# Attention's DVE and ACT order changed, its first batch normalised in halves, some of the final weighing moved to DVE, one batch's statistics moved

## What is computed

```python
x = x + 0.5 * ffn(layernorm(x))
x = x + attention(layernorm(x))
x = x + 0.5 * ffn(layernorm(x))          # the same weights as the first

def ffn(x):                               # 16 experts, top 2 of the 2 best of 4 groups, inner width 128
    s = softmax(x @ gate_w.T); pick 2 of s + gate_b in the two best groups; weights = s of the picked
    return sum over the 2 of weight * ((silu(x @ We1 + be1) * (x @ We3 + be3)) @ We2 + be2) \
         + (silu(x @ ws1 + bs1) * (x @ ws3 + bs3)) @ ws2 + bs2

def attention(x):                         # 16 heads of 16, linear attention
    q, k, v = relu(x @ Wq), relu(x @ Wk), x @ Wv
    z = 1 / (sum_n(k) . q + eps)
    return ((v^T k) q * z) @ w_proj.T + b_proj
```

## Time and profile before

| | |
|---|---|
| median of 3 runs | 1249.27 us (1247.13 to 1252.63) |
| the profiled execution | 1243.24 us, its span 1241.5 us |
| PE busy (matmul) | 1148.4 us, 93% |
| DVE busy | 852.7 us, 69% |
| ACT busy | 759.6 us, 61% |
| POOL busy | 698.1 us, 56% |
| DMA, mean | 146 GB/s; about 400 GB/s in the final stage |
| granted TensorE clock, mean | 0.982 of full |

### The profile page before, as it was taken

One profiled execution on the slowest core, in us unless ns is written; L12 is line 12 of the kernel. 1 busy time (PEld: TensorE's weight loads), 2 busy tenths in 40 slices (PEclk: granted clock), 3 DMA queues, 4 the chain that ended last, 5 costly groups with the idle time before them and its releaser, 6 DMA issues.

```text
span 1241.5 us, 26349 instructions
## 1 busy us (share of the span) xinstructions
PE 1148.4 (93%) x6696; PEld 904.6 (73%) x6696; DVE 852.7 (69%) x2774; ACT 759.6 (61%) x1698; POOL 698.1 (56%) x850
## 2 busy tenths in 40 slices
PE   7988999999999967899998999889998999999995
PEld 5555555899999946777887878545557999999653
DVE  6788784566666655768878786677844666666488
ACT  4454441688888845675655653544415888888398
POOL 3577776488888854000411503356763888887810
PEclk9999999999999998999999999899999999999997
DMA  9922227556555523012320400114585555555398
GB/s 360 309 91 95 98 104 201 172 172 174 171 172 156 164 104 105 32 38 68 112 72 24 133 22 35 35 69 141 171 210 180 173 170 174 173 157 162 119 400 333
DMA packets 94215, 181.53 MB, mean 146 GB/s; under 512 B 17624, under 2 KB 60400, under 8 KB 92022
## 3 DMA queue, kind: packets, MB, share of 16 engines
q1 hardware_dynamic: 66630, 110.44, 29.2%
q0 software_dynamic: 26016, 67.55, 15.3%
q10 hardware_dynamic: 1424, 1.86, 0.5%
HBM read 97.63 MB, written 86.08 MB: 148 GB/s over the span
## 4 chain that ended last, share of the span: by engine, by line
PE 58%; DVE 17%; ACT 11%; issue 5%; POOL 5%; DMA 3%; SPq 1%; DVEq 0%; ACTq 0%; POOLq 0%
PE bank L700 20%; PE bank L710 10%; PE bank L559 7%; PE bank L691 5%; POOL expert_rows L1683 4%; PE bank L575 4%; PE bank L806 3%; ACT rows L1021 3%; ACT w L1021 3%; DVE stat L1161 2%; PE bank L756 2%; PE bank L732 2%; ACT xn L1039 1%; PE bank L521 1%; ACT rows L898 1%
## 5 line engine op out<-in xcount | busy, mean ns | idle before, releaser
L700 PE MATMUL bank<-rows,att 128*128 128x128 f32 x2288 | 303.2, 276 | 0.3 <-ACT att L1010 0.3
L700 PEld LDWEIGHTS bank<-rows,att 128*128 128x128 f32 x2288 | 279.2, 192 | 0.8 <-ACT att L1010 0.6
L1683 POOL DMA_INDIRECT expert_rows<-rows,slots x160 | 155.4, 971 | 80.0 <-issue 57.3
L1010 ACT COPY att<-w 128x512 f32 x286 | 177.0, 619 | 10.2 <-issue 4.2
L1740 POOL DMA_INDIRECT routed_rows<-silu,rdest x160 | 158.3, 989 | 35.0 <-issue 24.6
L1458 DVE SCALAR_TENSOR_TENSOR rows<-bank,tile_b,att 128x128 f32<-128x128 f32 x286 | 100.1, 350 | 112.9 <-ACT att L1015 102.0
L710 PE MATMUL bank<-w,rows 128*128 x572 | 171.5, 382 | 4.3 <-DVE rows L1458 4.2
L1740 POOL DMA_INDIRECT routed_rows<-rows,rdest x126 | 124.7, 990 | 68.4 <-DVE rdest L1441 40.7
L1009 ACT COPY rows<-bank 128x256 f32<-128x256 f32 x286 | 106.6, 373 | 89.1 <-PE bank L691 86.9
L575 PE MATMUL bank<-ws,be 128*128 128x256 f32 x512 | 124.0, 388 | 8.6 <-DVE be L1364 8.6
L925 ACT ACTIVATE silu<-bank,bs 128x512 f32<-128x512 f32 x64 | 43.9, 686 | 127.6 <-PE bank L559 117.5
(11 more groups left out here) (212 smaller groups left out, 2156.9 us busy)
## 6 DMA issues: line engine op xcount, KB each, us to landing
rows<-expert_rows SPq DMA_DIRECT2D x286, 129.5 KB
rows<-routed_rows SPq DMA_DIRECT2D x32, 512.0 KB, 4.2
w<-routed_rows SPq DMA_DIRECT2D x10, 1024.0 KB, 10.9
out<-xres SPq DMA_DIRECT2D x16, 512.0 KB, 9.3
xres<-in_x SPq DMA_DIRECT2D x7, 1024.0 KB, 9.5
rows<-routed_rows SPq DMA_DIRECT2D x6, 1024.0 KB, 7.7
expert_rows<-pad SPq DMA_DIRECT2D x47, 129.5 KB, 14.0
w<-in_w SPq DMA_DIRECT2D x1, 4096.0 KB, 24.4
```

What stands on the lines that cost most here:

```text
L700: last = nc.tensor.matmul(rh_ps[t % RB][:, n * P:(n + 1) * P], m.rw13[:, t % RB, c * C + n * INTER:c * C + (n + 1) * INTER], m.rT[:, t % R ...
L1010: nc.scalar.copy(m.rw13[:, a % RB, :].rearrange("p (c n) -> p c n", c=KC), w13[:, :, bass.ds(expert_at(i + 2), C)]).then_inc(s.rw13_copied, 1)
L1683: nc.gpsimd.indirect_dma_start(out=d.xg, out_offset=bass.IndirectOffsetOnAxis(ap=m.slots[:, slots_of(r), k, i:i + 1], axis=0), in_=m.xs[bu ...
```

## The change

- In the attention periods 0 to 6, DVE no longer takes the statistics of the last pair of tiles ahead of the second half of the key sum, but behind it, with the aggregation.
- ACT's last two normalising instructions of a batch (`following(range(6, 8))`) stand behind the second copy of transposed queries, where they stood ahead of the mixer's copy.
- In the first batch the statistics, `rstd`, negated mean, normalising and transposes are done for tiles 0 to 3 first, and for tiles 4 to 7 later: ACT's second half stands behind its second relu, PE's behind the second Gram step. The four weighings of batch 1 stand behind ACT's relus 3 to 6, where they stood behind 0, 2, 4 and 6.
- In period 7, `route_stats(13)` stands behind `route_stats(11)`, ahead of `sum_keys(7, 0)`, with a semaphore of its own; it leaves the period's end.
- In final pieces 3, 7, 11 and 15, DVE weighs and adds the first of the two routed rows in one instruction for each tile (`scalar_tensor_tensor`), and ACT weighs only the second.

```diff
--- before.py
+++ after.py
@@ -291,6 +291,10 @@
 NEXT = BATCHES + EARLY
 
 
+def weighed_by_dve(n):
+    return 1 if n % 4 == 3 else 0
+
+
 def early_in(b, step):
 
     e, late = divmod(b - 1 - step, 2)
@@ -828,8 +834,8 @@
 
             pe.wait_ge(s.att_weights_in, 16 * len(att_loads))
             pe.wait_ge(s.bias_placed, 16)
-            for n in range(4):
-                a_transpose(0, n)
+            a_transpose(0, 0)
+            a_transpose(0, 1)
             keys(0, 0)
             keys(0, 1)
             for b in range(BATCHES):
@@ -843,6 +849,9 @@
                 keys(b, 2)
                 for i in range(NT):
                     gram(b, i)
+                    if b == 0 and i == 1:
+                        a_transpose(0, 2)
+                        a_transpose(0, 3)
                     if i + 3 < NT:
                         keys(b, i + 3)
                     if i == 5:
@@ -1015,8 +1024,8 @@
                         nc.scalar.activation(m.rsilu[:, t % RB, :], rh_ps[t % RB][:, 0:P], ACT.Silu,
                                              bias=m.tile_b13[:, 0, i:i + 1]).then_inc(s.rsilu_ready, 1)
 
-            def weigh(b, tiles, y):
-                for k in range(2):
+            def weigh(b, tiles, y, choices=range(2)):
+                for k in choices:
                     for j, i in enumerate(tiles):
                         last = nc.scalar.activation(y[:, k, j * C:(j + 1) * C], y[:, k, j * C:(j + 1) * C], ACT.Copy,
                                                     scale=m.weights[:, b, k, i:i + 1])
@@ -1030,10 +1039,14 @@
             def weigh_final(n):
                 b, h = divmod(n, PIECES)
                 act.wait_ge(s.f_loaded[n % FSLOTS], 16 * (n // FSLOTS + 1))
-                weigh(b, range(h * NT // PIECES, (h + 1) * NT // PIECES), m.yf[n % FSLOTS]).then_inc(s.f_weighted, 1)
+                weigh(b, range(h * NT // PIECES, (h + 1) * NT // PIECES), m.yf[n % FSLOTS],
+                      range(weighed_by_dve(n), 2)).then_inc(s.f_weighted, 1)
 
             def a_normalise(b, tiles):
-                act.wait_ge(s.a_nmr_ready, b + 1)
+                if b == 0 and tiles[0] < PAIRS:
+                    act.wait_ge(s.a_first_nmr, 1)
+                else:
+                    act.wait_ge(s.a_nmr_ready, b + 1)
                 wait(act, s.g_ready, b)
                 for i in tiles:
                     last = nc.scalar.activation(m.xn[:, i, :], m.xres[:, b, i, :], ACT.Identity,
@@ -1090,9 +1103,9 @@
 
             for h in range(PAIRS):
                 weigh_routed(0, h)
-            a_normalise(0, range(NT))
-            for n in range(4):
-                a_copy_xT(0, n)
+            a_normalise(0, range(0, PAIRS))
+            a_copy_xT(0, 0)
+            a_copy_xT(0, 1)
             for b in range(BATCHES):
                 more = b + 1 < BATCHES
                 fresh, ranked = early_in(b, 0), early_in(b, 1)
@@ -1103,7 +1116,15 @@
 
                 for i in range(NT):
                     relu_k(b, i)
-                    if more and i % 2 == 0:
+                    if b == 0:
+                        if i == 1:
+                            a_normalise(0, range(PAIRS, NT))
+                        if i == 3:
+                            a_copy_xT(0, 2)
+                            a_copy_xT(0, 3)
+                        if 3 <= i < 7:
+                            weigh_routed(1, i - 3)
+                    elif more and i % 2 == 0:
                         weigh_routed(b + 1, i // 2)
                     if fresh is not None and 3 <= i < 7:
                         normalise(fresh, range(2 * i - 6, 2 * i - 4))
@@ -1124,11 +1145,12 @@
                 relu_q(b, 2)
                 following(range(4, 6))
                 relu_q(b, 3)
-                following(range(6, 8))
                 act.wait_ge(s.mixer_ready, b + 1)
                 nc.scalar.copy(m.m_sb.rearrange("p c n -> p (c n)"), g_ps[:]).then_inc(s.mixer_copied, 1)
                 for p in range(PAIRS):
                     copy_qT(b, p)
+                    if p == 1:
+                        following(range(6, 8))
                     if more:
                         a_copy_xT(b + 1, p)
                     else:
@@ -1471,7 +1493,7 @@
                             dve.wait_ge(s.rows_out[last_user % SLOTS], 16 * (last_user // SLOTS) + 16)
                         TT(m.ry[(i - 2) % RYSLOTS], ry_ps[y % RB][:, 0:C], m.be2[:, bass.ds(e, C)], ALU.add).then_inc(s.ry_scaled, 1)
 
-            def combine(b, h):
+            def combine(b, h, measure=True):
                 n = PAIRS * b + h
                 y = m.ylq[:, n % YSLOTS]
                 dve.wait_ge(s.bias_added, BIASED.index(b) + 1)
@@ -1479,7 +1501,11 @@
                 dve.wait_ge(s.weighted, n + 1)
                 ch.then(TT(x, x, y[:, 0, :], ALU.add))
                 TT(x, x, y[:, 1, :], ALU.add).then_inc(s.combined, 1)
-                dve.wait_ge(s.combined, n + 1)
+                if measure:
+                    measure_sums(b, h)
+
+            def measure_sums(b, h):
+                dve.wait_ge(s.combined, PAIRS * b + h + 1)
                 stats(b, range(2 * h, 2 * h + 2))
 
             def a_negate_mean(b):
@@ -1574,10 +1600,14 @@
             for n in HELD[0]:
                 shared(0, n, iter(()), 0)
 
-            for h in range(PAIRS):
+            for h in range(PAIRS // 2):
                 combine(0, h)
-            aggregate(s.a_stats_ready)
-            a_negate_mean(0)
+            half_aggregate(0, s.a_first_stats)
+            combine(0, 2)
+            half_negate_mean(0, s.a_first_rstd, s.a_first_nmr)
+            combine(0, 3)
+            half_aggregate(1, s.a_stats_ready)
+            half_negate_mean(1, s.a_rstd_ready, s.a_nmr_ready)
             def steps(work, count):
                 for _ in range(count):
                     next(work, None)
@@ -1597,7 +1627,9 @@
                         steps(work, 1)
                     combine(b + 1, 1)
                 else:
-                    route_stats(BATCHES + EARLY)
+                    route_stats(NEXT)
+                    stats(NEXT + 2 - BATCHES, range(NT), m.early)
+                    aggregate(s.later_stats, m.early)
                 if ranked is not None:
                     steps(work, 1)
                 sum_keys(b, 0)
@@ -1605,12 +1637,14 @@
                     steps(work, 1)
                 if more:
                     combine(b + 1, 2)
-                    combine(b + 1, 3)
-                    aggregate(s.a_stats_ready)
+                    combine(b + 1, 3, measure=False)
                 else:
                     negate_mean(BATCHES + EARLY)
                     route_stats(BATCHES + EARLY + 1)
                 sum_keys(b, 1)
+                if more:
+                    measure_sums(b + 1, 3)
+                    aggregate(s.a_stats_ready)
                 scale(b, 0)
                 if more:
                     a_negate_mean(b + 1)
@@ -1640,8 +1674,6 @@
                 if ranked is not None:
                     for _ in slots(ranked):
                         pass
-                if not more:
-                    route_stats(NEXT + 2)
                 if b == 0:
                     route_stats(BATCHES)
                 elif following is not None:
@@ -1656,8 +1688,17 @@
                 for part in held_ahead(n):
                     shared(1, part, iter(()), 0)
                 dve.wait_ge(s.bias_added, BATCHES + BIASED.index(b) + 1)
-                dve.wait_ge(s.f_weighted, n + 1)
-                TT(x, x, y[:, 0, :], ALU.add).then_inc(s.f_added, 1)
+                if weighed_by_dve(n):
+                    dve.wait_ge(s.f_loaded[n % FSLOTS], 16 * (n // FSLOTS + 1))
+                    for j, i in enumerate(range(h * NT // PIECES, (h + 1) * NT // PIECES)):
+                        tile = m.xres[:, b, i, :]
+                        last = nc.vector.scalar_tensor_tensor(tile, y[:, 0, j * C:(j + 1) * C],
+                                                              m.weights[:, b, 0, i:i + 1], tile, ALU.mult, ALU.add)
+                    last.then_inc(s.f_added, 1)
+                    dve.wait_ge(s.f_weighted, n + 1)
+                else:
+                    dve.wait_ge(s.f_weighted, n + 1)
+                    TT(x, x, y[:, 0, :], ALU.add).then_inc(s.f_added, 1)
                 dve.wait_ge(s.f_added, 2 * n + 1)
                 TT(x, x, y[:, 1, :], ALU.add).then_inc(s.f_added, 1)
@@ -1667,7 +1708,10 @@
             small = dict(allow_small_or_imprecise_dtypes=True)
 
             def rstd(r):
-                pool.wait_ge(s.stats_ready, r + 1)
+                if r == NEXT + 2:
+                    pool.wait_ge(s.later_stats, 1)
+                else:
+                    pool.wait_ge(s.stats_ready, r + 1 - (r > NEXT + 2))
                 wait(pool, s.xn_half, normalised_of(r))
                 apart(pool, s.passed)
                 own = tiles_of(r)
@@ -1798,7 +1842,12 @@
```

(8 more changed lines are left out.)

1 line of the change is left out of this document (added).

## The result

| | before | changed |
|---|---|---|
| median of 4 runs each | 1248.28 us (1247.13 to 1252.63) | 1231.62 us (1228.77 to 1234.82) |
| the profiled execution, its span | 1243.24, 1241.5 us | 1234.82, 1232.8 us |
| granted TensorE clock, mean | 0.982 | 0.983 |

The ratio is 0.986 [0.984, 0.988]: 16.7 us less, where 16.65 were predicted.

The account below looks back on a forecast made before the run. PE was taken to bound the kernel, with 58% of the chain of waits (DVE 17%). Terms: 10.35 - 0.7 + 3.4 + 1.6 + 2.0 = 16.65 us; 1249.27 - 16.65 = 1232.6 us, range 1225 to 1242.

Parts of the forecast that it names:

- First period, 2.85: Period 0: 1.85 us at L770 from the halves and key sum's order, plus 1.0 from the last two normalisings.
- keys start at about 471.0 ... So far 5 us are gained: First batch, in halves: keys start at about 471.0 instead of 477.5; keys 4 begin at 477.7 against 482.8.
- The addition that was to last 2 to 3 us beside POOL: Period 0: DVE's first addition of `combine(1, 0)` is held up until POOL's 26 additions end, lasting 2 to 3 us.
- The rival of an unhindered DVE: POOL's additions don't hold DVE up: period 0 gives 4.1 us, total gain 19 to 20.5, time 1229 to 1230; chance 0.20.
- a stretch at 0.50 within period 0: Listed sign that the prediction is wrong: granted PE clock at its lower level, 1.2 GHz, somewhere in period 0.
- the slower outcome: Period 0 wholly at 1.2 GHz: +34.8 us, change 18 us slower, 1267; decides from about 16 us of such work; chance 0.03.
- Key sum, 1.5 in periods 2, 4 and 6: DVE's key sum ahead of the last statistics and aggregation: gains 1.5 us in each of these periods, nothing in 1, 3, 5.
- Last two normalisings, 1.0: ACT's last two normalisings behind the second copy: PE's wait of 1.21 falls to 0.2, 1.0 us in periods 0, 2, 4, 6.
- Period 7 and its end, -0.7, 3.4 and 1.6: Moved statistics overrun DVE's wait by 0.7 us; 3.4 go at period 7's end; clock staying at 2.4 GHz there gives 1.6.
- "Given back to the clock", the rival at 0.15: Clock falls behind batch 11's selection (3.4 us back, 1.6 not won), key sum's gain halved (-2.3): gain 9.4, time 1240; chance 0.15.
- Final stage, 2.0: DVE weighs one row in four pieces, 0.35 us per new instruction: its last addition ends 2.0 us sooner, bounds 0.5 and 3.5.
- The range: Whole kernel: 1225 to 1242 us, from best unhindered case (1229) to given-back case (1240), with 2 to 3 either side.

Follow-up runs that it names:

- e11: The changed kernel without any edit, measured again on a later occasion: ratio to the kernel before 0.9876, median 1230.44 us.
- e10: The changed kernel with ten more of POOL's additions put ahead of its first `rstd`, PE not kept busy: ratio 0.9875, 1230.12 us.
- e8: The changed kernel with 46 unused matmuls on PE ahead of the first batch and ten more POOL additions ahead of the first `rstd`: ratio 0.9815, 1223.82 us.
- e4: The changed kernel with batch 5's statistics put back to the end of period 7: ratio 0.9891, 1233.44 us.
- e5: The changed kernel with all weighing of the final stage on ACT again: ratio 0.9855, 1226.10 us.
- e6: The changed kernel with 46 unused matmuls on PE ahead of attention's first transposes: ratio 0.9846, 1225.34 us.
- e7: The changed kernel with POOL's 26 additions held back to run beside DVE's additions of batch 1: 1229.76 us, one run, no ratio.
- e2: The changed kernel with the key sum put back behind the last statistics and the aggregation: ratio 0.9917, 1237.17 us.
- e1: The changed kernel with the first batch's halves undone: ratio 0.9863, 1230.02 us.
- e3: The changed kernel with ACT's last two normalisings put back ahead of the mixer's copy: ratio 0.9890, 1232.93 us.
- e9: e8 with the fourth weighing behind relu 7 and, in period 0, the second key sum ahead of the fourth `combine`: ratio 0.9821, 1223.69 us.

## Why the prediction was right, and where it was not

**Total.** 1232.6 us was predicted and 1231.62 measured. The sum of 16.65 agrees with the medians (16.7; 15.9 in e11's runs) better than with the profiles (13.1 and 14.5). Part of that is the profile of before, which was itself 5 us under its kernel's median; about 1.5 of the 5 lay in layer 1, which ended at 458.25 where the twelve other profiles, with the same code there, have a median of 459.8, and where the rest lay wasn't settled. The agreement to 1 us is therefore luck in good part. In the profile after, periods 1 to 7 gave 2.4 us more than predicted, and period 0 and the clock stretch behind the selection of batch 11 gave 3.1 less. What it does show is which steps held.

**First period, 2.85.** It gave 1.5 in the profile after and 2.1 in e11. The step that failed is "keys start at about 471.0 ... So far 5 us are gained". The first key was to come 6.5 us sooner and came 5.5 sooner here, 6.5 in e11, but I priced the keys with the duration of before, and their place in the clock's recovery had moved: 5.17 for 2.75 is 2.4 us. The addition that was to last 2 to 3 us beside POOL took 0.69, because those 2.4 us let POOL finish. The other half of that chain held: a load that landed 3.8 us behind the additions and PE's wait behind the fourth weighing set the period's pace. What the slow keys cost can be read from profiles side by side. The first four have the same code up to the end of period 0; e10 moves POOL's row, e8 also brings the clock up.

| profile | first key sooner | twelve keys | low clock ends behind the first key | gained in period 0 |
|---|---|---|---|---|
| after | 5.5 | 5.17 | 4.7 | 1.5 |
| e11 | 6.45 | 5.49 | 5.5 | 2.1 |
| e4 | 6.5 | 5.14 | 4.7 | 2.5 |
| e5 | 6.6 | 4.38 | 3.1 | 3.3 |
| e10 | 5.6 | 4.46 | 3.3 | 2.3 |
| e8 | 6.3 | 2.86 | not low | 4.6 |

In each row the gain is the first column, less what the keys took over 2.75, less 1.6. So a microsecond of slow keys costs period 0 a microsecond, and 2.85 is no wrong figure for this code but one of a spread from 1.5 to 3.3 that the clock decides; that it lies inside is luck, as it was reached with a blocked addition and fast keys, neither of which came. In e6 the keys are fast and 3.9 us more are missing: the stay of 1.8, a load that landed 4.4 behind the additions, and up to 1.7 from the clock's fall at 494.01. The rival of an unhindered DVE (4.1 at L770) was right about the addition and wrong about the gain there (0.5 to 2.3); the blocking it denied is real, as e6 shows, and e8 shows what its removal gives when the keys are fast: 3.6 at L770. My list called a stretch at 0.50 within period 0 a wrong sign, and there was one, 4.7 us of the first keys. It never reached the 16 us from which the slower outcome would have decided.

The Trainium skill ("SBUF — State Buffer", Who interferes with whom) says that the engine that issues first holds the shared pair for its instruction and the other fully blocks. e7 agrees: POOL's addition grew from 0.45 to 0.90 or more beside a DVE addition of 0.69, and neither stayed out for more than about one instruction of the other. e6 and the earlier trace rows show more than the rule gives: in e6 DVE stayed out for about four POOL instructions on end (2.47 minus 0.69 is 1.8 us of additions of 0.41), not for one.

**Key sum, 1.5 in periods 2, 4 and 6.** Right; 1.70 by e2. The size: I added busy times (0.67 and 0.86), and the gaps between the instructions were missing. DVE's timeline has the moved block in one piece, behind the key sum of period 0:

```profile
497.09 0.42 DVE L1523 TENSOR_TENSOR rows<-att 128x256 f32<-128x256 f32 x1
497.55 0.75 DVE L1183 BATCH_NORM_STATS2 stat<-xres 128x6 f32<-128x256 f32 x2
498.34 0.64 DVE L1189 BATCH_NORM_AGGREGATE mv<-stat 128x2 f32<-128x6 f32 x8
499.02 0.17 DVE L1191 TENSOR_SCALAR ve<-mv 128x8 f32<-128x8 f32 x1
499.21 0.69 DVE L1537 TENSOR_TENSOR att<-be,att 128x512 f32<-128x512 f32 x1
```

From 497.55 to 499.21 it is 1.66 us.

**Last two normalisings, 1.0.** Right in the even periods (0.97), and 0.38 in each odd one and 0.65 in the last were missed: 1.8 us. I had priced only the wait that carried that label.

**Period 7 and its end, -0.7, 3.4 and 1.6.** Right: -0.63 by e4, and 5.0 for the two others together. The clock stayed up there, the term that I had been least sure of.

**"Given back to the clock", the rival at 0.15.** Half of it came true: the clock fell at 802.08, behind PE's waits of 1.74 and 1.22, and took back 1.7 us, in both profiles of the changed kernel. In e4, e5, e6 and e10 it took back 3.1, nearly the rival's 3.4, and in e1, e3, e7 and e9 nothing. The sum had nothing for it.

**Final stage, 2.0.** 1.5 in the profile after. The new instruction takes 0.42 each (1.66 for four), not 0.35: 0.3 us more for each of four pieces, two of which (11 and 15) stand where DVE has no wait left. As DVE's timeline shows none from 1211.1 on, the end goes by its work alone. In e11 only 0.2 was left of it: its clock was at 0.50 from 1211.9 to 1218.8, PE's last part of the shared expert took 6.72 for 5.41, and DVE waited 1.23 for it, which is nearly all of the 1.3 that are missing. e4 shows the same stretch, a wait of 1.27 and the 0.2, and the eight other profiles with DVE's weighing show 1.5. This wasn't tested by an experiment of its own, and the times don't show the gain of this stage (e5).

**The range.** Its lower end, 1225, is 4 us under the 1229 that it is said to follow from by 2 to 3.

## What to carry to other kernels

Price work that is moved forward by the clock it will then run at, not by its old duration: the 5.5 to 6.6 us won on the first key bought 1.5 to 3.3, because the keys now ran at 1.2 GHz, and only a busy PE ahead of them (e6) together with POOL's row out of the way (e8) brought 4.6. Where two instructions are put behind others in a stream, look at every consumer of what they pass, in every kind of period; the waits that carry their label in the old trace are only part of it. Gains of up to 3 us here were decided by whether a clock stretch fell and how long it was, so they have to be read from marks in several traces, not from one span.

## What was unexpected of the hardware

- DVE's large additions and POOL's row of additions side by side don't always fare alike. In e7 they alternate, DVE 0.83 for 0.69, POOL 0.90 to 1.01 for 0.45, also where POOL's row was already running (0.92 at 498.15). In e6 (2.47) and the earlier trace rows (1.52) DVE's addition ends 0.5 us behind the row. Why is open.
- The same stage with the same waits ran at either clock: L565 x8 behind waits of 1.74 and 1.23 took 3.67 in e1 and 5.37 behind 1.74 and 1.22 in the changed kernel, and 6.64 in e5, whose code is the changed kernel's up to there.
- `scalar_tensor_tensor` on 128x256, all operands in SBUF, takes 0.42 us in a row of four (1.66), a third more than its share of one addition of 128x1024 (1.23).
- The first rows of the experts of layer 3 kept PE waiting 3.53 us (after), 1.71 (e11) and 1.21 (before); the first two are of the same code.
